# A windowed attention and a mixture of experts on one core: the attention moved one slot forward, key blocks copied by halves of the partitions, scaled input on ACT, the experts' biases transferred ahead of their chunks

## What is computed

```python
x = L0_attn_x
x = x + _L0_attn_ref(_layernorm(x), ...)   # attention block
x = x + _L0_ffn_ref(_layernorm(x), ...)    # experts block

# attention block
h = _layernorm(x, norm1_g, norm1_b)
qkv = h @ qkv_w + qkv_b                    # 16 heads of 16
scores = q . k over a window of 15 keys, / 4; softmax; times v
x = shortcut + (out @ proj_w + proj_b)
m = _layernorm(x, norm2_g, norm2_b)
x + gelu(m @ fc1_w + fc1_b) @ fc2_w + fc2_b    # hidden size 1024

# experts block, per row
main = gelu(x @ W1m + b1m) @ W2m + b2m
top 2 of 8 experts from softmax(mean(x) @ w_gate + b_gate)
a * main + (1 - a) * sum over both of gate * (gelu(x @ W1e + b1e) @ W2e + b2e)
```

## Time and profile before

| | |
|---|---|
| time, median of 3 runs | 2036.63 us (2033.87 to 2037.24) |
| time of the profiled execution | 2034.47 us |
| its span, first to last instruction | 2032.7 us |
| mean granted TensorE clock | 0.997 |
| PE busy | 1989.9 us, 98% of the span |
| DVE busy | 1498.7 us, 74% |
| ACT busy | 1098.8 us, 54% |
| POOL busy | 1116.4 us, 55% |
| DMA | 108.82 MB, mean 54 GB/s |

### The profile page before, as it was taken

How to read it: one execution, slowest core, us unless ns; L and a number is a source line. 1 busy time by engine, 2 the same in 40 slices (tenths; PEclk the granted TensorE clock), 3 DMA queues, 4 the chain that set the end, 5 groups by cost and what they waited for, 6 DMA issues and landing times.

```text
span 2032.7 us, 37549 instructions
## 1 busy us (share of the span) xinstructions
PE 1989.9 (98%) x13478; PEld 1816.7 (89%) x13478; DVE 1498.7 (74%) x2449; ACT 1098.8 (54%) x1733; POOL 1116.4 (55%) x976
## 2 busy tenths in 40 slices
PE   7989999999999999999999999999999999999999
PEld 6789999999998999989999999899989989899998
DVE  7577687876868678686876878768686786868743
ACT  4455555555555465565555555554554555655554
POOL 7556275563755636465562755637556464655625
PEclk9999999999999999999999999999999999999999
DMA  3121111211102121121211112111021211212121
GB/s 105 47 63 48 47 53 32 73 53 52 53 28 73 47 63 53 40 60 37 73 53 44 51 32 74 53 52 53 30 74 44 63 53 42 58 37 74 42 58 53
DMA packets 188851, 108.82 MB, mean 54 GB/s; under 512 B 65437, under 2 KB 187641, under 8 KB 188665
## 3 DMA queue, kind: packets, MB, share of 16 engines
q1 hardware_dynamic: 188088, 105.62, 18.3%
q10 hardware_dynamic: 576, 0.79, 0.1%
HBM read 85.52 MB, written 8.39 MB: 46 GB/s over the span
## 4 chain that ended last, share of the span: by engine, by line
PE 68%; DVE 19%; issue 7%; ACT 4%; POOL 1%; DMA 0%; SPq 0%; DVEq 0%; ACTq 0%; POOLq 0%
PE psB L232 34%; PE psA L232 24%; DVE hr_lo L550 5%; PE psA L1048 3%; PE psA L1075 3%; PE psA L969 2%; DVE smax L624 2%; DVE tm L641 2%; PE psA L1060 2%; DVE qm L593 1%; DVE smax L617 1%; DVE pr L628 1%; DVE pr L609 1%; ACT pr L874 1%; DVE acc L566 1%
## 5 line engine op out<-in xcount | busy, mean ns | idle before, releaser
L550 DVE TENSOR_TENSOR hr_lo<-hf,hr_hi 128x512 fp32r<-128x512 f32 x512 | 495.6, 968 | 431.2 <-ACT hr_hi L841 430.6
L841 ACT ACTIVATE hr_hi<-hf 128x512 fp32r<-128x512 f32 x512 | 323.7, 632 | 266.4 <-PE psB L232 179.3
L437 POOL TENSOR_TENSOR wx_lo<-raw,wx_hi 128x512 fp32r<-128x512 f32 x256 | 398.5, 1557 | 21.3
L450 POOL TENSOR_SCALAR kb<-kT,gmask 128x384 f32<-128x384 f32 x128 | 174.9, 1381 | 302.8 <-ACT kT L857 302.8
L435 POOL TENSOR_SCALAR wx_hi<-raw 128x512 fp32r<-128x512 f32 x256 | 195.6, 764 | 250.5 <-PE psB L232 239.8
L232 PE MATMUL psB<-wx_hi,hr_hi 128*128 128x256 f32 x1024 | 289.1, 282 | 0.4 <-DVE hr_lo L550 0.2
L232 PE MATMUL psB<-wx_hi,hr_lo 128*128 128x256 f32 x1024 | 286.4, 280 | 0.0
L232 PE MATMUL psB<-wx_lo,hr_hi 128*128 128x256 f32 x1024 | 285.7, 279 | 0.0
L837 ACT ACTIVATE hf<-psB,b1x 128x512 f32<-128x512 f32 x256 | 174.8, 683 | 181.2 <-PE psB L232 168.3
L232 PE MATMUL psB<-z_hi,wx_hi 128*128 128x512 f32 x512 | 211.8, 414 | 0.0
L232 PEld LDWEIGHTS psB<-wx_hi,hr_hi 128*128 128x128 f32 x1024 | 192.5, 188 | 15.3 <-DVE hr_lo L550 6.7
(11 more groups left out here) (150 smaller groups left out, 5207.7 us busy)
## 6 DMA issues: line engine op xcount, KB each, us to landing
raw<-in_L_ffn_W1e SPq DMA_DIRECT2D x256, 128.0 KB, 2.2
raw<-in_L_ffn_W2e SPq DMA_DIRECT2D x256, 128.0 KB, 2.2
out_x<-acc SPq DMA_DIRECT2D x32, 256.0 KB, 2.2
xin<-in_L_attn_x SPq DMA_DIRECT2D x15, 512.0 KB, 3.8
vb<-vs SPq DMA_DIRECT2D x64, 96.0 KB
vb<-vs SPq DMA_DIRECT2D x64, 80.0 KB
tm<-in_L_ffn_b2e SPq DMA_DIRECT2D x32, 128.0 KB, 3.1
raw<-in_L_attn_fc_w SPq DMA_DIRECT2D x8, 256.0 KB, 3.6
```

The lines of the kernel that those rows point to most:

```text
L437: g.tensor_tensor(wx[1][:, s, :], raw[:, s, :], wx[0][:, s, :].bitcast(f32), ALU.subtract).then_inc(w_lo.sem, 1)
L450: g.tensor_scalar(kb[:, th, :, gr * KW:(gr + 1) * KW], win, gmask[:, gr:gr + 1], None, ALU.mult).then_inc(kb_s.sem, 1)
L550: v.tensor_tensor(hr[1][:, c % 2, :], hf[:, c % 3, :], hr[0][:, c % 2, :].bitcast(f32), ALU.subtract).then_inc(h_lo.sem, 1)
L841: a.activation(hr[0][:, c % 2, :], hf[:, c % 3, :], ACT.Copy).then_inc(h_hi.sem, 1)
```

## The change

1. **Ladders.** In stages with attention the steps from `turn(0)` on stand one slot earlier on all engines: `turn(0)` in slot 4 instead of 5, `scores(2)` in 5 instead of 6, `attend(0)` and `turn(1)` in 6 instead of 7, and so on to the second norm's transposes in 16 instead of 17. `scores(0)`, `scores(1)` and the projections in slots 0 to 3 stay, as do slots 19 and on. On DVE `normalise(0)` goes ahead of the low part of chunk 3, `normalise(1)` from slot 4 to 3, and `route_bias` from slot 5 to slot 2.
2. **Key blocks.** Each of the four instructions of a `keys` call works on 64 partitions instead of 128, and with constants instead of `gmask`; the zero halves are written once by DVE at the start. POOL waits for each of them before it starts the next one.
3. **Scaled input.** The four instructions that make `y` move from POOL (subtract and multiply) to ACT (scale and bias, slot 5). DVE makes the bias `nb` in one small instruction a row. The sum with `bproj` stays on POOL, as `norm1_bias`.
4. **Biases.** `chosen` issues its four transfers ahead of the first chunk's weights instead of behind the fourth's.
5. **Stage 0.** `WARM` has 73 matmuls instead of 95. `hmask` is made ahead of the first powers, `gmask` is gone.

```diff
@@ SP
                             n, s, e, c = loads, loads % RING, loads // KH, loads % KH
-                            if n == RING:
+                            if n == 0:
                                 chosen(f, ex)
-                                if t < ROWS:
-                                    windows(t)
+                            elif n == RING and t < ROWS:
+                                windows(t)
@@ POOL, constants (hmask now ahead of the first row's powers, gmask gone)
-            g.wait_ge(dzero.sem, 6)
+            g.wait_ge(dzero.sem, 7)
@@ POOL keys(t, c)
                     for gr in range(G):
-                        g.tensor_scalar(kb[:, th, :, gr * KW:(gr + 1) * KW], win, gmask[:, gr:gr + 1], None, ALU.mult).then_inc(kb_s.sem, 1)
+                        first = kT[64 * gr:64 * gr + 64, th * UB * QB:th * UB * QB + 1]
+                        win = bass.AP(first.tensor, first.offset, [first.ap[0], [QB, UB], [1, KW]])
+                        g.tensor_scalar(kb[64 * gr:64 * gr + 64, th, :, gr * KW:(gr + 1) * KW], win, 1.0, 0.0, ALU.mult, ALU.add).then_inc(kb_s.sem, 1)
+                        g.wait_ge(kb_s.sem, kb_s.at(t, 2 * u + gr))
@@ POOL norm1_y becomes norm1_bias (only the sum with bproj), at q 7 instead of 8; power(t, 1) at q 14 instead of 15
-                for i in range(NT):
-                    g.tensor_scalar(y[:, i, :], xin[:, i, :], mv[:, 0, i, 0:1], rs[:, i:i + 1], ALU.subtract, ALU.mult).then_inc(y_s.sem, 1)
@@ DVE
-            zeros = [kT[:, 0:LEFT], kT[:, LEFT + T:ZW]]
+            zeros = [kT[:, 0:LEFT], kT[:, LEFT + T:ZW], kb[:, :, :, :].rearrange("p h b k -> p (h b k)")]
+            def shifts(row):
+                v.wait_ge(*((rstd[0].sem, rstd[0].at(row - 1)) if row else (rstd_first.sem, rstd_first.all(0))))
+                if row:
+                    v.wait_ge(y_s.sem, y_s.all(row - 1))
+                v.scalar_tensor_tensor(nb[:, :], mv[:, 0, :, 0], -1.0, rs[:, 0:NT], ALU.mult, ALU.mult).then_inc(nb_s.sem, 1)
...
-                    if q == 10 and t < ROWS:
-                        normalise(t, 2)
-                    elif q == 16 and t < ROWS:
-                        norm2_apply(t, 1)
+                    if t < ROWS:
+                        if q == 3:
+                            normalise(t, 0)
+                        elif q == 9:
+                            normalise(t, 2)
+                        elif q == 15:
+                            norm2_apply(t, 1)
                     if q < NQ and there(ORDER[q][0], t):
                         h_low(t, *ORDER[q], q)
...
+                    elif q == 2 and f >= 0:
+                        route_bias(f)
                     elif q == 3 and t < ROWS:
-                        normalise(t, 0)
+                        normalise(t, 1)
                     elif q == 4 and t < ROWS:
                         query_blocks(t, 2)
-                        normalise(t, 1)
-                    elif q == 5 and f >= 0:
-                        route_bias(f)
-                    elif q == 6 and t < ROWS:
+                    elif q == 5 and t < ROWS:
                         mask(t, 2)
                         shift(t, 2)
...
@@ ACT
+            def norm1_y(t):
+                if t:
+                    a.wait_ge(sx_s.sem, sx_s.at(t - 1))
+                a.wait_ge(nb_s.sem, nb_s.at(t))
+                for i in range(NT):
+                    a.activation(y[:, i, :], xin[:, i, :], ACT.Identity, bias=nb[:, i:i + 1], scale=rs[:, i:i + 1]).then_inc(y_s.sem, 1)
...
-                    elif q == 5:
+                    elif q == 4:
                         turned(t, 0)
                         query_blocks(t, 3)
-                    elif q == 7:
+                    elif q == 5:
+                        norm1_y(t)
+                    elif q == 6:
                         turned(t, 1)
...
@@ PE
-            WARM = {1: 10, 4: 14, 5: 5, 6: 3, 8: 4, 9: 10, 10: 6, 11: 3, 12: 4, 13: 14, 15: 14, 17: 8}
+            WARM = {1: 10, 3: 5, 4: 3, 5: 5, 8: 11, 10: 3, 11: 4, 12: 12, 14: 12, 16: 8}
...
+                    elif q == 4:
+                        turn(t, 0)
                     elif q == 5:
-                        turn(t, 0)
+                        scores(t, 2)
                     elif q == 6:
-                        scores(t, 2)
-                    elif q == 7:
                         attend(t, 0)
                         turn(t, 1)
+                    elif q == 7:
+                        scores(t, 3)
...
```

More of the change, by code:

```diff
@@ L109, in build @@
         hmask = sb("hmask", [P, HS])
-        gmask = sb("gmask", [P, G])
+        nb = sb("nb", [P, NT])
         hbias = sb("hbias", [P, KD, HS])
@@ L398, in power @@
                 g.tensor_tensor(rs[:, to:to + ww], ve[:, lo:lo + ww], mhalf[:, 0:ww], ALU.pow).then_inc(rstd[n].sem, 1)
+            const(g.memset(hmask[:, :], 1.0))
+            for h in range(2):
+                v = hmask[64 * h:64 * h + 64, :]
+                const(g.affine_select(out=v, in_=v, compare_op=ALU.is_ge, fill=0.0, base=0, pattern=[[-HD, HS]], channel_multiplier=1))
+                const(g.affine_select(out=v, in_=v, compare_op=ALU.is_ge, fill=0.0, base=HD - 1, pattern=[[HD, HS]], channel_multiplier=-1))
+            assert made == N_CONST, made
             for j, (a_, b_) in ((1, EXTRA[1]), (0, EXTRA[0])):
@@ L407, in _ @@
                     g.tensor_tensor(rs[:, j * NT + lo:j * NT + hi], ve[:, j * NT + lo:j * NT + hi], mhalf[:, 0:hi - lo], ALU.pow).then_inc(rstd_first.sem, 1)
-            const(g.memset(hmask[:, :], 1.0))
-            for h in range(2):
-                v = hmask[64 * h:64 * h + 64, :]
-                const(g.affine_select(out=v, in_=v, compare_op=ALU.is_ge, fill=0.0, base=0, pattern=[[-HD, HS]], channel_multiplier=1))
-                const(g.affine_select(out=v, in_=v, compare_op=ALU.is_ge, fill=0.0, base=HD - 1, pattern=[[HD, HS]], channel_multiplier=-1))
-            const(g.memset(gmask[:, :], 1.0))
-            const(g.affine_select(out=gmask[:, 0:1], in_=gmask[:, 0:1], compare_op=ALU.is_ge, fill=0.0, base=63, pattern=[[0, 1]], channel_multiplier=-1))
-            const(g.affine_select(out=gmask[:, 1:2], in_=gmask[:, 1:2], compare_op=ALU.is_ge, fill=0.0, base=-64, pattern=[[0, 1]], channel_multiplier=1))
-            assert made == N_CONST, made
             g.memset(vb[:, :, :, :, :], 0.0).then_inc(zeroed.sem, 1)
-            g.wait_ge(dzero.sem, 6)
+            g.wait_ge(dzero.sem, 7)
             g.wait_ge(rows_in.sem, rows_in.all(0))
@@ L441, in keys @@
                     u = 2 * c + th
-                    first = kT[:, th * UB * QB:th * UB * QB + 1]
-                    win = bass.AP(first.tensor, first.offset, [first.ap[0], [QB, UB], [1, KW]])
                     g.wait_ge(kT_s.sem, kT_s.at(t, c))
@@ L486, in _ @@
                             weights(8, 10)
-                            norm1_y(0)
+                            norm1_bias(0)
                             weights(10, 13)
-                    elif q == 8 and t:
-                        norm1_y(t)
-                    elif q == 15:
+                    elif q == 7 and t:
+                        norm1_bias(t)
+                    elif q == 14:
                         for h in range(2):
@@ L721, in _ @@
             gained_T(0, tr1, t1_f1, t1_hi, t1_lo, 1, oG1, oB1)
+            shifts(0)
             v.wait_ge(consts.sem, N_CONST)
@@ L791, in _ @@
                         norm1_z(t + 1)
+                        shifts(t + 1)
                     elif q == SPLIT + 8 and t + 1 < ROWS:
@@ L926, in _ @@
                             weights_high(12, 13)
+                    elif q == 10:
+                        turned(t, 2)
                     elif q == 11:
-                        turned(t, 2)
+                        turned(t, 3)
                     elif q == 12:
-                        turned(t, 3)
-                    elif q == 13:
                         attended_high(t, 1)
@@ L1138, in _ @@
                         project_qk(t, 1, 0, 3)
+                    elif q == 4:
+                        turn(t, 0)
                     elif q == 5:
-                        turn(t, 0)
+                        scores(t, 2)
                     elif q == 6:
-                        scores(t, 2)
-                    elif q == 7:
                         attend(t, 0)
                         turn(t, 1)
+                    elif q == 7:
+                        scores(t, 3)
                     elif q == 8:
-                        scores(t, 3)
-                    elif q == 9:
                         attend(t, 1)
+                    elif q == 10:
+                        turn(t, 2)
                     elif q == 11:
-                        turn(t, 2)
-                    elif q == 12:
                         attend(t, 2)
                         turn(t, 3)
-                    elif q == 13:
+                    elif q == 12:
                         attend(t, 3)
```

39 lines of the change are left out of this document (17 added, 22 removed).

## The result

The changed kernel takes 2018.58 us (median of 4 runs, 2016.80 to 2020.90), the kernel before 2035.25 us (4 runs). The ratio is 0.9919, with a 95% interval of 0.9902 to 0.9936: faster by 0.8%. The profiled execution took 2019.08 us with a span of 2017.4 us.

A forecast was written before the change was run, and what follows sets the result against it. PE, busy 98% of the span, was taken as the bound, so only its waits could be won. Full stages 15.9 us plus stage 0's 3.1 made 19.0 off the median 2036.63: 2017.6, rounded to 2018 us, range 2012 to 2024.

The forecast's parts named there:

- The stages: Full stages: of 1.41 us PE loses, 1.41 - 0.1 - 0.25 = 1.06 is won, times 15 = 15.9 us.
- the stall at `turn(1)`: PE between `attend(0)` and `turn(1)`, waiting for `mask(2)` behind `route_bias` on DVE: the 0.82 us lost per stage goes.
- At `scores(2)`: PE wants `scores(2)` a slot earlier, just before DVE's query blocks are ready: a new wait of about 0.1 us.
- At `turn(2)`: PE in slot 10, waiting for `gather` and `normalise(2)` on DVE: a wait of 0.25 us kept, bounds 0 and 0.59.
- Stage 0: Start-up stage, paced by the chain through DVE: 3.1 us sooner, about 2 from `normalise(3)`'s product; bounds 0 and 6.
- For PE this is worth nothing: Key blocks on POOL: about 0.6 us each instead of 1381 ns, but PE has them in time even at the old price.
- the danger: POOL's two-input L437, moved earlier, could meet a low part on DVE, which took 1.75 us instead of 0.69 beside it.
- Biases ahead: Four transfers issued before the first chunk's loads: loads start 2 to 3 us later, biases land before `route_bias`; no effect.
- `y` on ACT: Four instructions of 128x256 ahead of chunk 6: 1.9 us, bounds 1 and 3; even 3 us are covered.
- (a): Rival: `route_bias` stays at 3.74 us on DVE, `scores(2)` waits 0.75; 9.3 us gained, 2027 us; chance 0.14.
- (b): Rival: `route_bias` at 3.74 and chunk 4's low part at 1.75 beside L437; slower, 2044.6 us; chance 0.08.
- (c): Rival: ACT delivers chunk 5 too late, so `mask(2)` still holds `turn(1)`; 2033 to 2036 us; chance 0.08.

The follow-up runs named there:

- the wait of the key blocks: Changed kernel, with a stage's third and fourth key block on POOL waiting until DVE's product of `normalise(1)` is done: median 2015.37 us, ratio 0.9898.
- the combined kernel: Changed kernel plus the wait of the key blocks in every stage, and more filler and `turn(2)` behind `up(11)` in stage 0 alone: ratio 0.9882.

## Why the prediction came out right

**The stages: right, by the mechanism.** I said 1.06 us a full stage, times 15, 15.9; measured are 1.11 and 15.7. `route_bias` cost 2.19, ended ahead of both `normalise`, and the stall at `turn(1)` went. It was 0.74 and not 0.82: I had set `attend(0)` at the 1.70 of `scores(2)`, and it takes 1.78 where nothing waits. At `scores(2)` I said 0.1 us of new wait. What the wait of the key blocks gave is 0.19 a stage, with the changed kernel in its shorter outcome, and in the longer one it is 0.35 to 0.4 more; in the profiled execution that was so in three stages. At `turn(2)` I said 0.25, and 0.35 are left. The step there was right (`gather` stands ahead of `normalise(2)`, which ends at 1016.48). By my own sum 1.41 - 0.19 - 0.35 = 0.87 would be left. The starts of PE's instructions (medians of the full stages, before against after) give 0.74 at `turn(1)`, 0.25 at `turn(2)`, 0.21 between `turn(2)` and `attend(2)`, and -0.18 around `scores(2)`: 1.02, so 0.1 stays unassigned. The 0.21 is the late low part shown above, which I had not looked for. It makes up for the terms that I had too good, so that the sum came closer (1.06 against 1.11) than its terms.

**Stage 0: the term that was mis-sized.** I said 3.1 us sooner; measured is 0.3 later in the profiled execution and 0.5 sooner in the second one. With all profiles of either stage 0, the mean is 116.2 after (five) and 116.5 before (two): some 0.3 us sooner, with a scatter of 1 to 2 us, and not 3.1. The product of `normalise(3)` did fall from 3.08 to 0.96. DVE and POOL of stage 0 show where part of it went:

```profile
51.40 1.17 DVE L621 TENSOR_TENSOR pr<-pr,rinv 128x768 f32<-128x768 f32 x1
52.49 1.75 DVE L640 TENSOR_TENSOR zT_lo<-tm,zT_hi 128x512 fp32r<-128x512 f32 x1
...
55.43 0.96 DVE L621 TENSOR_TENSOR pr<-pr,rinv 128x768 f32<-128x768 f32 x1
```

```profile
47.34 3.18 POOL L455 TENSOR_TENSOR y<-y,bproj 128x1024 f32<-128x1024 f32 x1
50.47 4.91 POOL L424 TENSOR_TENSOR wf_lo<-raw,wf_hi 128x512 fp32r<-128x512 f32 x3
```

With `y` gone, POOL comes sooner to its two-input splits. They meet DVE's low part `zT_lo` (1.75 us; before, beside `y`, 0.69) and the product ahead of it (1.17; before 0.96), so 1.3 of the 2.1 us went back at once. `turn(3)` starts at 56.44 instead of 57.07, and the last transposes of the stage at 110.49 instead of 110.92. PE in stage 0 shows the second part. With less filler it stood idle ahead of `scores(2)`:

```profile
35.90 2.13 PE L1061 MATMUL psA<-kb,qm 128*128 128x96 f32 x16 [1.81 <-DVE qm L586]
...
40.02 2.46 PE L1088 MATMUL psA<-pT,vb 96*128 96x128 f32 x16
```

`scores(2)` started 1.65 us sooner than before, `attend(0)` at 40.02 against 40.03, since the granted clock fell to 0.50 between 38 and 40 us. This is not bound to happen: with `route_bias` in slot 4, after the same idle time of 1.82 us, the clock stayed at 1.00 there, and `attend(0)` came at 38.98. It fell behind `turn(2)` instead (2.61 us idle, clock 0.56 between 54 and 56 us), where the changed kernel after 2.60 us idle kept 1.00. At the stage's end, after 3.93 us idle (before, 3.72), PE ran with a granted clock of half for a while. First after, then in the combined kernel, whose filler stands there:

```profile
110.00:117.00 7.00, 6.51 (x29) 6.28 (x30) 3.10 (x10) 1.85 (x6) 0.00 (x0) 0.56 0.00 0
```

```profile
110.00:117.00 7.00, 7.00 (x55) 6.69 (x56) 3.62 (x12) 2.68 (x7) 0.00 (x0) 1.00 0.04 11
```

From the last transposes to the search it takes 5.70 us after, 4.96 before (clock 0.76 in the same window) and 3.69 in the combined kernel (clock 1.00). For these two profiles stage 0 is -0.43 in the chain and +0.74 behind it, +0.31 in all. But the same stretch took 5.01 to 5.71 us in the five profiles of the same stage 0, so the 0.74 are not the change's. What is shown is that the idle time at the stage's end costs 1.3 to 2.0 us before and after alike, and that filler takes it away. I had priced only the instruction that became shorter, and had neither asked what POOL does in the time that it gains nor whether PE, idle for longer with less filler, would keep its clock. How much of the missing 2.8 us falls to each of the two is open.

**The rest.** *"For PE this is worth nothing"* of the key blocks was right for their price (122.26 us with the old form) and wrong for their place: 0.35 us a stage hang on which of two instructions comes first. I had seen the danger one instruction later, at the low part, for L437; the new instruction that met DVE's was the key block itself. The Trainium skill, SBUF — State Buffer, section "SBUF: two separate sides", says that the shared port pair goes to whichever of the two starts first, for its whole instruction. The trace agrees: 0.96 and 1.33 us one way round, 1.30 and 0.51 the other, and which way it goes follows the starts down to 5 ns (above). The memset of `vb`, of which I said by the same section that it would hold up nothing, ran from 12.80 to 16.31, and the two low parts beside it took their usual 0.7 each:

```profile
13.27 1.47 DVE L563 TENSOR_TENSOR zT_lo<-pT,zT_hi 128x512 fp32r<-128x512 f32 x2
```

*Biases ahead* went as said: issue at 974.67, `windows` again 9.2 us long. I had priced it for a full stage only; the 6.4 us of the last stage would have been the dearest place to get it wrong. `y` on ACT took 2.06 where I had 1.9, and hid. Of the rivals, (a) and (b) needed `route_bias` at 3.74, and it took 2.19. (c) needed ACT 1.2 us later; chunk 5's low part started at 997.21, and `turn(1)` at 1000.52 did not wait. The forecast of 2018 is right because the stages, where 15 equal terms add up, were read well. Its stage 0 was about 3 us too good. That the median of 2018.58 still lies 0.6 us from it is luck: I had subtracted 19.0 us from 2036.63, and the kernel before has 2035.25 in the four runs of the result, from which it would be 2016.3. The median of all nine runs of the changed kernel is 2019.88.

## What to carry to other kernels

An instruction with two SBUF inputs on DVE has the price that its neighbour on POOL gives it: `route_bias` took 2.2, 3.7 and 5.5 us in three places. So move it to where POOL waits, and, for every edit that changes when POOL runs, list what DVE does at that moment, down to ties of 0.01 us. When a stage's length has two values in one trace, look for two instructions that start together, and make one wait for the other if nobody needs it soon. Where filler stands in for work, a chain that gets shorter leaves PE idle for longer, and the clock may fall behind it; count the filler again. And before a difference in a start-up stage is explained, look how much that stage differs between executions of the same code.

## What the runs showed of the hardware

- A tie between DVE and POOL is decided anew in each stage, by starts that differ by a few ns, and for long stretches the same way: in the changed kernel twelve of 15 one way, with the unchanged full stages behind more filler 13 of 15 the other. Fifteen times 0.35 are 5.3 us, the size of the spread of the changed kernel's runs (2017 to 2023.5), and with the tie removed four runs lay within 2.1 us. That it makes the whole spread isn't shown, since the kernel before spreads by 5.4 us over 14 runs.
- A wait of PE of 3.9 us cost 6 us in one profiled execution, since the granted clock was at half in the five us behind it. After 1.8 us idle in stage 0 the clock fell to 0.50 in one profile and stayed at 1.00 in another of the same code; after 2.6 us it fell in the second and stayed in the first. Waits of 1.2 us at `turn(3)` left the mean clock of that kernel at 1.00.
- A key block of 64 partitions and 384 elements took 0.51 us undisturbed, with constants as scalars; the one of 128 partitions with a scalar from memory 1.25 undisturbed.
